# A gated cross-attention block over eight samples: the first sample computed on whole 32-bit values, low halves written over the raw values, and the second sample's first product moved ahead

## Reference

```python
def xattn(inp_q, inp_k, inp_v, Wt, Wp, Wg, Wz, gn_w, gn_b):   # q = layernorm(x), k = v = ctx
    t = einsum('oc,bcd->bod', Wt, inp_v)
    p = einsum('oc,bcd->bod', Wp, inp_q)
    g = einsum('oc,bcd->bod', Wg, inp_k)
    att = sum over each of 8 groups of (p * g)
    y = einsum('goi,bgid->bgod', Wz, att * t)
    return group_norm(y) * gn_w + gn_b + inp_v

def ffn(x, A_w, B_w, Wq_w, keys):              # 64 experts of rank 8, the 16 best are kept
    scores = x @ Wq_w.T @ keys.T
    gate = softmax over the top 16, zero elsewhere
    z = (x @ A_w.T) * gate (each expert's 8 columns)
    return z @ B_w.T * 2

x = x + tanh(g_xattn) * xattn(layernorm(x), ctx, ctx, ...)
x = x + tanh(g_ffn) * ffn(layernorm(x), ...)
```

## Time and profile before

| | |
|---|---|
| median of 3 runs | 371.48 us (370.81 to 372.13) |
| the profiled execution | 369.46 us, span from first to last instruction 367.6 us |
| PE busy | 336.3 us, 91% of the span |
| DVE / ACT / POOL busy | 285.3 / 159.8 / 151.1 us |
| mean granted TensorE clock | 0.963 of full speed |
| bytes moved | 47.50 MB, mean 129 GB/s |

### The profile page before, as it was taken

One profiled execution on the slowest core, in us unless ns is written; L12 is line 12 of the kernel. 1 busy time (PEld: TensorE's weight loads), 2 busy tenths in 40 slices (PEclk: granted clock), 3 DMA queues, 4 the chain that ended last, 5 costly groups with the idle time before them and its releaser, 6 DMA issues.

```text
span 367.6 us, 5693 instructions
## 1 busy us (share of the span) xinstructions
PE 336.3 (91%) x2104; PEld 307.9 (84%) x2104; DVE 285.3 (78%) x670; ACT 159.8 (43%) x257; POOL 151.1 (41%) x98
## 2 busy tenths in 40 slices
PE   5972996939699999999999999999999999999996
PEld 5871886728599889988999889988998899988984
DVE  2986489987868896898869896889689895787352
ACT  4690391751823445417612563344541761136110
POOL 0061178524476164553477067526455248000000
PEclk9995698978999999999999999999999999999999
DMA  7970571064721445062804173153606240001102
GB/s 265 406 263 32 203 256 57 0 235 123 247 84 57 171 157 189 0 229 75 270 3 156 74 220 126 59 171 139 206 1 230 67 164 0 2 1 59 57 29 87
DMA packets 14924, 47.50 MB, mean 129 GB/s; under 512 B 1824, under 2 KB 1952, under 8 KB 14896
## 3 DMA queue, kind: packets, MB, share of 16 engines
q1 hardware_dynamic: 14544, 46.93, 36.4%
q10 hardware_dynamic: 352, 0.20, 0.2%
HBM read 38.74 MB, written 8.39 MB: 128 GB/s over the span
## 4 chain that ended last, share of the span: by engine, by line
PE 75%; DVE 12%; DMA 5%; ACT 3%; issue 2%; POOL 1%; SPq 1%; ACTq 0%; DVEq 0%
PE w_ps L899 23%; PE z_ps L872 23%; PE w_ps L790 9%; PE w_ps L821 9%; PE t_ps L860 4%; DVE B_lo L532 3%; PE z_ps L833 3%; DMA uw<-in_cT 3%; PE w_ps L872 2%; PE t_ps L886 2%; DMA raw<-in_xT 1%; DVE u_st L581 1%; DMA raw<-in_cT 1%; PE t_ps L803 1%; DVE x_st L547 1%
## 5 line engine op out<-in xcount | busy, mean ns | idle before, releaser
L276 POOL TENSOR_TENSOR xT_lo<-raw,xT_hi 128x1024 fp32r<-128x1024 f32 x14 | 41.9, 3014 | 37.6 <-ACT xT_hi L358 37.6
L899 PE MATMUL w_ps<-B_hi,zT_hi 128*128 128x512 f32 x128 | 53.5, 418 | 2.4 <-issue 2.4
L899 PE MATMUL w_ps<-B_hi,zT_lo 128*128 128x512 f32 x128 | 50.7, 396 | 0.0
L899 PE MATMUL w_ps<-B_lo,zT_hi 128*128 128x512 f32 x128 | 50.6, 395 | 0.0
L872 PE MATMUL z_ps<-A_hi,hT_hi 128*128 128x288 f32 x224 | 49.2, 302 | 0.0
L872 PE MATMUL z_ps<-A_lo,hT_hi 128*128 128x288 f32 x224 | 48.7, 300 | 0.0
L872 PE MATMUL z_ps<-A_hi,hT_lo 128*128 128x288 f32 x224 | 48.5, 298 | 0.0
L872 PEld LDWEIGHTS z_ps<-A_hi,hT_hi 128*128 128x128 f32 x224 | 37.1, 193 | 0.6
L872 PEld LDWEIGHTS z_ps<-A_hi,hT_lo 128*128 128x128 f32 x224 | 36.8, 192 | 0.0
L872 PEld LDWEIGHTS z_ps<-A_lo,hT_hi 128*128 128x128 f32 x224 | 36.7, 192 | 0.0
L281 POOL TENSOR_TENSOR cT_lo<-raw,cT_hi 128x1024 fp32r<-128x1024 f32 x12 | 28.7, 2392 | 16.6 <-DVE uw L629 16.6
(11 more groups left out here) (147 smaller groups left out, 868.7 us busy)
## 6 DMA issues: line engine op xcount, KB each, us to landing
c_sb<-in_ctx SPq DMA_DIRECT2D x16, 512.0 KB, 4.5
raw<-in_xT SPq DMA_DIRECT2D x16, 512.0 KB, 5.3
x_sb<-in_x SPq DMA_DIRECT2D x16, 512.0 KB, 3.2
out_block<-uw SPq DMA_DIRECT2D x14, 512.0 KB, 2.9
raw<-in_cT SPq DMA_DIRECT2D x12, 512.0 KB, 4.0
uw<-in_cT SPq DMA_DIRECT2D x4, 512.0 KB, 7.9
raw<-in_aT SPq DMA_DIRECT2D x4, 256.0 KB, 5.8
raw<-in_bT SPq DMA_DIRECT2D x4, 256.0 KB, 4.3
```

The lines of the kernel that those rows point to most:

```text
L276: pool.tensor_tensor(xT_lo[:, half_of(h), :], raw[:, half_of(h), :], xT_hi[:, half_of(h), :].bitcast(f32), ALU.subtract).then_inc(xT_lo_s, 1)
L899: last = pe.matmul(w_ps[k][:, :], z[:, t, row], w[:, j, cols], start=(j == 0 and z is zT_hi and w is B_hi), stop=(j == KN - 1 and z is zT_lo))
```

## The change

Four things change together.

1. **Sample 0 on whole values.** Wu, ctx, xT, cT, Wp and M of sample 0 are no longer split; PE multiplies the plain 32-bit values, one product where three stood (`first_u`, `first_gram`, `first_n`). Its high and low parts disappear from ACT and DVE. Wu and Wp are still split for the later samples.
2. **Raw values in place of low halves.** `split` lays the raw values where the low part will be, so a low part overwrites its own raw values. The lots, and the xT and cT of sample 1, need no wait before their load; `c_sb` becomes two buffers. The first xT and cT lie where `B_hi` comes later.
3. **New orders.** `u_product(1)` stands before the first z product. On PE the products of sample 1 change places; POOL takes the low parts of eight lots (A 4 to 7, B 0 to 3) and cuts its 1024-wide operations in pieces of 512; in the steady loop POOL no longer waits for `w_done` before a low part, and DVE's `offsets(m)` comes after the last `add_out`.
4. **Transposes of the identity** (`keep_busy`): 24 of them from the moment the identity is there, 8 more behind the Wu products. Nothing reads their result.

```diff
+        def split(name, shape):
+            hi = sb(f"{name}_hi", shape, f32r)
+            with nc.sbuf_tensor(f"{name}_in", shape, f32) as raw:
+                pass
+            return hi, sb(f"{name}_lo", shape, f32r), raw
...
+            def load_transposes(n):
+                for h in range(NH):
+                    if n >= 2 and h == 0:
+                        sp.wait_ge(gram_done, per_tile(n - 1, T - 1))
+                    sp.dma_start(xT_raw[:, half_of(h), :], xT[n][:, half_of(h), :]).then_inc(xT_in[h], 16)
+                    sp.dma_start(cT_raw[:, half_of(h), :], cT[n][:, half_of(h), :]).then_inc(cT_in[h], 16)
...
             load_c(0)
+            load_x(0)
             load_first_transposes()
-            load_x(0)
-            sp.dma_start(wp_nat, wpT).then_inc(wp_in, 16)
+            load_c(1)
+            sp.dma_start(Wp_raw[:, :, :], wpT).then_inc(wp_in, 16)
             sp.dma_start(Wg_sb[:, :, :], wg).then_inc(wg_in, 16)
-            for j in range(KD - 2):
+            for j in range(KD):
                 load_lot(j)
-            load_cT(0, 1)
...
+            load_transposes(1)
+            for j in range(KD, KD + KN):
                 load_lot(j)
             load_x(1)
...
         def _(act):
+            act.wait_ge(wu_done, 1)
+            act.activation(Wu_first[:, :, :], z_ps[0][:, :].rearrange("p (t c) -> p t c", t=T), ACT.Copy).then_inc(wu_s, 1)
             c_high(0, 0)
-            act.wait_ge(wu_done, 1)
-            act.activation(Wu_hi[:, :, :], z_ps[0][:, :].rearrange("p (t c) -> p t c", t=T),
-                           ACT.Copy).then_inc(wu_hi_s, 1)
...
         def _(dve):
             x_stats(0)
-            for h in range(NH):
-                dve.wait_ge(xT_hi_s, per_tile(0, h))
-                dve.tensor_tensor(xT_lo[:, half_of(h), :], raw[:, half_of(h), :],
-                                  xT_hi[:, half_of(h), :].bitcast(f32), ALU.subtract).then_inc(xT_lo_s, 1)
...
         def _(pe):
+            def first_u():
+                pe.wait_ge(wu_s, 1)
+                for k in range(USES):
+                    t, cols = use(k)
+                    for c in range(T):
+                        if k == 0:
+                            pe.wait_ge(c_in[c], 16)
+                        last = pe.matmul(w_ps[k][:, :], Wu_first[:, c, t * P:(t + 1) * P], c_sb[0][:, c, cols],
+                                         start=(c == 0), stop=(c == T - 1))
+                    last.then_inc(u_done, 1)
...
+            def keep_busy(times):
+                for _ in range(times):
+                    pe.transpose(w_ps[3][:, 0:P], ident[:, :], ident[:, :])
+            pe.wait_ge(ident_done, 1)
+            keep_busy(24)
             pe.wait_ge(wt_in, 16)
             pe.wait_ge(wz_in, 16)
...
+            keep_busy(8)
+            first_u()
+            pe.wait_ge(mean_const, GPT)
+            ctx_sums(0)
+            first_gram()
+            group_means(0)
             pe.wait_ge(wq_in, 16)
...
             last.then_inc(router_done, 1)
-            pe.wait_ge(ident_done, 1)
-            pe.wait_ge(mean_const, GPT)
-            pe.wait_ge(wu_lo_s, 1)
-            u_product(0)
-            ctx_sums(0)
-            gram(0, lambda: None)
-            group_means(0)
-            pe.wait_ge(wp_lo_s, 1)
-            n_product(0)
-            group_att_var(0)
+            first_n()
+            u_product(1, lambda: group_att_var(0))
             pe.wait_ge(router_lo_s, 1)
             hT(0, 0)
-            hT(1, 0)
...
+            z_product(0, 0, z_ps, lambda: hT(1, 0), KN - 2)
+            pe.wait_ge(u_copied, per_use(1, USES - 1))
+            z_product(1, 0, w_ps[NH:USES])
+            zT(0, 0)
+            gram(1, lambda: ctx_sums(1))
+            group_means(1)
+            out_product(0, 0)
+            n_product(1)
+            zT(1, 0)
+            out_product(1, 0, lambda: group_att_var(1))
+            out_product(2, 0, lambda: hT(0, 1))
+            out_product(3, 0, lambda: hT(1, 1))
```

More of the change, by code:

```diff
@@ L506, in _ @@
                 if nn < NB:
-                    for h in range(NH):
-                        cT_high(h, nn)
+                    xT_high(1, nn)
+                    cT_high(1, nn)
                 w_square(m)
@@ L593, in att_reduce @@
                                                     op1=ALU.add, accum_out=att_var[:, t:t + 1])
-                    step(last)
+                    last.then_inc(att_rows, 1)
             def group_deviation(n):
@@ L732, in _ @@
                               A_hi[:, :, NN:ZC].bitcast(f32), ALU.subtract).then_inc(router_lo_s, 1)
-            hT_low(0, 0)
-            for j in range(3, KD):
-                lot_low(j)
-            hT_low(1, 0)
-            for b in range(NB - 1):
+            lot_low(0)
+            dve.wait_ge(wg_in, 16)
+            att_reduce(0)
+            lot_low(1)
+            slopes(0, lambda: lot_low(2))
+            w_tiles(0)
+            hT_low(0, 0)
+            lot_low(3)
+            u_statistics(1)
+            hT_low(1, 0)
+            offsets(0)
+            gate(0, 0)
+            dve.wait_ge(wp_hi_s, 1)
+            dve.wait_ge(n_done, 1)
+            dve.tensor_tensor(Wp_lo[:, :, :], Wp_raw[:, :, :], Wp_hi[:, :, :].bitcast(f32), ALU.subtract).then_inc(wp_lo_s, 1)
+            x_stats(1)
+            minus_means(1)
+            gate(1, 0, w_ps[NH:USES])
+            zT_low(0, 0)
+            gram_fix(1)
+            M_low(1)
+            group_deviation(1)
+            for j in range(KD + KN, N_LOTS):
+                lot_low(j)
+            att_reduce(1)
+            zT_low(1, 0)
+            slopes(1)
+            w_tiles(1)
+            add_out(0, 0)
+            add_out(1, 0)
+            hT_low(0, 1)
+            add_out(2, 0)
+            hT_low(1, 1)
+            add_out(3, 0)
+            offsets(1)
+            for b in range(1, NB - 1):
                 m = b + 1
@@ L762, in _ @@
                 w_tiles(m)
-                offsets(m)
                 add_out(0, b)
@@ L769, in _ @@
                 add_out(3, b)
+                offsets(m)
             gate(0, NB - 1)
@@ L779, in _, with first_gram @@
         def _(pe):
+            def first_gram():
+                for t in range(T):
+                    for k in range(KD):
+                        if k % KH == 0 and t == 0:
+                            pe.wait_ge(first_xT_in[k // KH], 16)
+                            pe.wait_ge(first_cT_in[k // KH], 16)
+                            if k == 0:
+                                pe.wait_ge(wu_s, 1)
+                        last = pe.matmul(gram_bank(0, t)[:, 0:C], xT_first[:, k, t * P:(t + 1) * P], cT_first[:, k, :],
+                                         start=(k == 0), stop=(k == KD - 1))
+                    last.then_inc(gram_done, 1)
             def gram(n, between):
@@ L824, in u_product, with first_n @@
                     last.then_inc(u_done, 1)
+                    if k == 0 and middle:
+                        middle()
+            def first_n():
+                pe.wait_ge(wp_in, 16)
+                pe.wait_ge(M_hi_s, per_tile(0, T - 1))
+                for t in range(T):
+                    for c in range(T):
+                        last = pe.matmul(z_ps[0][:, t * C:(t + 1) * C], Wp_raw[:, c, t * P:(t + 1) * P],
+                                         M_first[:, c, :], start=(c == 0), stop=(c == T - 1))
+                last.then_inc(n_done, 1)
             def n_product(n):
-                pe.wait_ge(M_lo_s, per_tile(n, T - 1))
-                if n > 0:
+                pe.wait_ge(M_lo_s, from_second(n, T - 1))
+                if n == 1:
+                    pe.wait_ge(wp_lo_s, 1)
+                else:
                     pe.wait_ge(zg_done, per_tile(n - 1, T - 1))
```

415 lines of the change are left out of this document (191 added, 224 removed).

## The result

The changed kernel takes 344.81 us (median of 4 runs, 343.75 to 345.15). The kernel before, run beside it, takes 371.14 (370.39 to 372.13). The ratio is 0.9284, with a 95% interval of 0.9253 to 0.9315. The prediction was 345.

A forecast was written before the change was run, and what follows sets the result against it. PE was taken to bound the kernel, with only its start's waits and low clock to gain: 99.48 - 73.4 = 26.1 us saved, 343.4 profiled, 345 predicted for the median; range 338 to 355.

The forecast's parts named there:

- the sum: Whole kernel: PE's steps end the start at 73.4 instead of 99.48, saving 26.1 us, so 343.4 profiled.
- the signs of being wrong: PE waiting for POOL's low parts between 45 and 60, a wait before hT each round, low clock past 14 us.
- the case that the step chose: Start, first u product: from near 10.0 it takes 7.0 us at full clock, ending at 17.0.
- the better one it named: Start: the clock rises during the first transposes, making everything some 1.7 us earlier.
- rival 4: Start: clock stays low into the gram and transfers are late, so little is saved; 355 to 368 us, chance 0.04.
- Width by width from the 128-wide row: PE price of whole 32-bit products: 0.22 us for 128 columns, 0.44 for 256, 0.88 for 512.
- The lower bound: PE price of whole products: two passes at the fp32r rate, 0.46 us for 512 columns.
- the 5 us and more that were named: Start, before z(0,0): the time PE would idle without u(1) there as cover.
- The 2.5 us: End of the start: allowance for sample 1's slope chain arriving late, taken between 0.4 and some 4 us.
- 3 us of slack: Start: POOL's last cT (48.3) and last lot (53) come 3 us before PE needs them (51 and 56).
- Rival 1: Start slower than summed, from late POOL low parts or a clock drop: ends at 78 to 82, 350 to 354, chance 0.14.
- Rivals 2 and 3: Steady rounds: collision stretches each 0.5 to 1.5 us, 348 to 354, chance 0.14; or slower than before, chance 0.02.

The follow-up runs named there:

- experiments 1 and 2: The changed kernel without any transposes of the identity, 344.90 us; and the kernel before with only those 24 and 8 transposes added, 370.51 us.
- Experiment 4: The changed kernel with u(1), its DVE statistics and ACT copies put back behind gram(1): 349.20 us.
- experiment 5: The changed kernel with sample 1's xT and cT loads held for three lot low parts, and B lots for xT's low parts: 349.90 us.
- experiment 8: The changed kernel with the high and low parts of sample 0's zT put ahead of sample 1's exponentials and gate: 344.13 us.
- experiment 6: The changed kernel with each GpSimd low part one operation 1024 wide again, not two of 512: 350.98 us.
- Experiment 7: The changed kernel with GpSimd in the loop waiting for w_tiles again before the low part of xT: 344.54 us.

## Why the prediction was right, by its own steps

**The total.** Predicted 345, measured 344.81. The gain was predicted to lie in the start alone, and it does: 24.6 us of start, nothing in the rounds. The start was predicted to end at 73.4 and ends at 74.87; the profiled time is 344.88 against 343.4 by the sum. The median agreed better than the sum did because the sum's 1.5 us error met the 2.0 us that I had added for the profiled execution lying below the median. After the change the two are the same. So the last 1.5 us of the agreement are luck. The signs that were named for being right all came: z(0,1) between 70 and 77, whole 512-wide products 6.95/8 = 0.87 us apart, no wait of PE over 1.80 us behind 10 us, rounds under 40.2. Of the signs of being wrong one came, the low clock past 14 us (0.66 from 57 to 62).

**Transposes, Wu, u(0).** u(0) was predicted to start at 10.0 and end at 17.0; it ran from 8.73 to 15.84. The 24 transposes took 5.38 us (5.2 predicted), but Wu behind them took 1.26 and not 2.04: the clock had risen under the transposes. That lies between the case that the step chose (u(0) at full clock from 10.0) and the better one it named, and rival 4 is refuted. The measured time shows no gain from the transposes (experiments 1 and 2).

**Price of whole products.** u(0) 7.11 us (7.0 predicted), the gram 7.07 (7.0), n(0) 1.97 (1.8). Width by width from the 128-wide row was the right choice. The lower bound, two passes, is out.

**Up to z(0,0).** Router at 23.25 (24.5 predicted), transposes of `uw` at 32.73 (33.8), z(0,0) at 34.74 (35.7), means of sample 1 behind the gram at 55.30 (55.9). They are 1.3 to 0.6 us early, the 1.3 us of u(0) carried along and slowly used up. That u(1) just covers the slope chain of sample 0 held: PE's gap there is 0.98. Experiment 4 puts 4.4 us on it, of the 5 us and more that were named. That PE waits for no transfer held as well, as long as they are sent early (experiment 5, 5.1 us). They are less loose than the step had it: from 8.6 to 34.3 us they move 400 GB/s without a pause, and the first half of xT of sample 1 had landed by 28.4 us, 1.5 us before ACT took it.

**From the gram to z(0,1).** This is the step that was mis-sized: 15.0 + 2.5 = 17.5 us predicted, 74.87 - 55.46 = 19.4 measured. The 2.5 us were put on the slope chain of sample 1. Only 0.34 us of waiting was there. What came in its place is the wait for `zT_lo` (1.80), which the prediction didn't have, and the low clock behind it, which made out 0 take 4.46 us (57.38 to 61.84) in place of 2.74: together 3.9 us where 2.5 stood. The slope chain was hidden behind this, not absent. With the wait for `zT_lo` taken away (experiment 8) PE waits 1.16, 0.77 and 0.35 us for `B_lo`, the att sums and `uw`, 2.3 us of the 2.5. The cause that was named, DVE and GpSimd taking turns, was right, but not its place. The four `B_lo` ran undisturbed (2.49), because they came only after GpSimd was through; the small operations were hit, each held up by about 1 us by a 512-wide piece. The sum had priced a collision by the work of both engines, which for an operation on 2 elements gives nothing. Its price is the rest of the other engine's instruction, as experiment 6 shows by doubling the piece (1.2 to 2.16 us). The rule of the Trainium skill that was weighed there (SBUF — State Buffer, Who interferes with whom) has it that way, the second to issue being blocked until the first is done, and the trace agrees for `a` (1.21 us) and, in experiment 6, for `u_dev` (2.16), which read two operands from SBUF.

**GpSimd.** 20 us from 33 to 53 were predicted for its low parts, with 3 us of slack. Measured are 21.9, from 33.46 to 55.34. The cT low part, predicted at 48.3, was ready at 50.34, and the last lot, predicted at 53, at 55.34. PE took the one at 50.48, after a gap of 0.1 us, and was through with the gram at 55.46. So PE hardly waited for either, but the 3 us of slack were all used. Rival 1, which set the 20 us against 12 before, had the 12 too low: six operations of 2.39 us are 14.3.

**The rounds.** The collision of `xT_low` with `w_tiles` was predicted at 2.2 us on DVE and nothing on PE. It is 1.07 on the slope and 0.99 on `w_tiles`, 2.1 us, and the rounds take 39.94 to 39.99 us. Experiment 7 shows that taking it away gives nothing. Rivals 2 and 3 are refuted.

**Where the 24.6 us came from.** Undoing one part at a time costs 4.4 us (place of u(1)), 5.1 (early loads), 6.2 (cut pieces, 3.0 of it in the start), 3.1 (whole gram) and 0 (transposes). These are prices of undoing, not shares, and needn't add up. ACT still copies the ctx of sample 0 into `c_hi`, for its row sums; nothing reads the copy. What whole values for u(0), n(0) and Wu bring, and the other new orders, was not run by itself.
